# A decoder with two expert layers: the first expert layer turns its sorted tiles four at a time, runs its shared experts last and splits its weights on GpSimd

## The chip, the cores and the metric

The program runs on one core of a Trainium2 chip: one launch computes the whole decoder. The metric is the time of the device in microseconds (us). The engines are TensorE (PE; its loading of weights is shown apart as PEld), VectorE (DVE), ScalarE (ACT), GpSimd (POOL) and SyncE, whose queue (SPq) issues nearly all plain transfers. Each engine runs its instructions in order, and they wait for each other by semaphores.

## What is computed

A batch of 32 sequences of 64 tokens (2048 tokens, 256 features) goes through six blocks: a rotary recurrence, a cross attention, a first expert layer, a linear attention, a quantised cross attention and a second expert layer. The change touches the third alone. What that one computes, with `x` after a layer norm without weights:

```python
score = sigmoid(xn @ wa)                                  # 16 routed experts
val, idx = top_k(score, 2); val = val / val.sum(-1)
y_e = gelu(xn @ g_e + gb_e) * (xn @ w1_e + b1_e)           # [tokens, 128]
out_e = y_e @ w2_e + b2_e
x = x + xn + out_shared0 + out_shared1 + sum(val_k * out_(idx_k))
```

(`x + xn` since the layer's input is added again inside it.) Each token passes through its two chosen routed experts and through both shared ones.

## The kernel before

The stage is `experts_top2`. Tokens stand in 16 tiles of 128 (`NT`), in four blocks of 512 (`NBLK`, `TPB` = 4 tiles in a block). Products run in f16 with every operand split in a high part (scaled by 1024) and a low part: `split_product` is six matmuls, high by high, high by low and low by high, each over two halves of the features.

**Norm** (`RowNorm`): VectorE takes the moments of 16 tiles, ScalarE the square root (L904), and then, for each block b, VectorE writes `xn`, ScalarE its high part (L907) and VectorE its low part (`low`, L884) into `rows`, which lie in `xnT`. SyncE turns each finished block with one transposing DMA into `xh` or `xl` (L916) and copies it to `rows_dram` (L917).

**Routing** (`Dispatch`): TensorE's logits, ScalarE's sigmoid (L982), VectorE's choice of two experts (`vector_choose`), counts by TensorE (`tensor_place`) and places by VectorE (`vector_place`, to L1057). The routed work is sorted: each expert's tokens fill whole tiles of 128 rows, 48 tiles in all (`TILES`), in 12 quads of four. `vector_hot` and `tensor_list` make, for the first and the second choice in turn, the list `token` of which token sits in which row (L1075 to L1080), and `vector_experts` the expert of each tile.

**Weights**: 18 experts (16 routed, 2 shared) come through three staging slots (`Wgu`, `Wd`). ScalarE writes high parts (`split_high`, L1228 and L1229), VectorE low parts (`weights_low`, L1330 and L1331), from the staged f32 in one operation each. The order is written out by hand: the two shared experts first, then two experts after each shared step.

**Shared experts**: eight steps (2 experts by 4 blocks): `shared_up` (12 matmuls of 512 columns), `gate` and `hidden` (gelu on ScalarE, product on VectorE), high and low part of the result (`hidden_high`, `low`), `shared_down` (4 tiles by 4 matmuls of 256 columns, of which the fourth adds a bias: `ones3` by `b2r`, 3 partitions each), and `add` into `X`. These steps run while the weights of the routed experts still arrive and while the routing is computed.

**Routed experts**: GpSimd gathers each of the 48 tiles from `rows_dram` into one of four one-tile buffers `got` (`RING`, L1212), SyncE turns it into one of two quad buffers `XG` (L1188), and a gather into a buffer waits for the turn out of it. Per quad TensorE loads four expert numbers (`value_load`) and runs 48 matmuls of 128 columns (`routed_up`) and 16 of 256 (`routed_down`). ScalarE and VectorE empty the result into `y` (`take`), and SyncE keeps it in `y_dram` (`keep`). After the twelfth quad GpSimd gathers 32 tiles back into eight buffers `G` (L1220), and VectorE adds each, weighted, into `X` (L1382).

## Time and profile before

| | us |
|---|---|
| median of 3 runs (lowest, highest) | 2793.87 (2790.25, 2794.61) |
| the profiled execution, its own time | 2792.5 |
| its span | 2790.4 |
| this stage, from its first DMA issue to the end of its last operation | 475.8 to 754.0 |
| of that, until the first shared matmul | 475.8 to 518.3 |
| the shared steps | 518.3 to 593 |
| the twelve routed quads | 593.7 to 707.5 |
| gathering back and adding | 707.5 to 754.0 |
| mean granted clock of TensorE over the span, of full speed | 0.786 |

Times in the rows below are microseconds from the span's start. In a timeline row the first number is the start and the second the duration. For a row of several instructions (x4, x48) it is from the first start to the last end. A bracket says how long the engine had been idle before, and what ended that; "issue" means that nothing the profile shows did. A matmul's duration is longer than the distance to the next one, since they are pipelined: distances between starts tell TensorE's pace.

### The profile page before, as it was taken

How to read it: one execution, taken by the hardware profiler on the slowest of the kernel's cores; microseconds unless marked ns; L12 is line 12 of the kernel's file. 1: busy time of each engine (PE TensorE's matmuls, PEld its weight loads, DVE VectorE, ACT ScalarE, POOL GpSimd, SP SyncE). 2: the span in 40 equal slices, each digit the busy share in tenths (PEclk: the TensorE clock that was granted, in tenths of full speed). 3: DMA queues.
4: the chain of work that ended last, by engine and by line, in shares of the span. 5: the costliest groups of instructions: out<-in, count | busy, mean ns of one | idle time of the engine just before them, and what ended most of it. 6: DMA issues, size and time to landing. Idle time of an engine off the chain costs nothing. (4 is left out here: it accounts for less than half of the span.)

```text
span 2790.4 us, 44150 instructions
## 1 busy us (share of the span) xinstructions
PE 2067.5 (74%) x15822; PEld 1219.5 (44%) x15822; DVE 1742.4 (62%) x3183; ACT 1402.6 (50%) x1950; POOL 972.2 (35%) x882
## 2 busy tenths in 40 slices
PE   6783776487189999999946366666666549999998
PEld 3332554245067777777745122222222234444444
DVE  6996564742333333333365899999999645666665
ACT  4562332232043333333323488888888525666664
POOL 0000220023423223232313588888888600101010
PEclk9996777688589999999977555555555569999999
DMA  3000000468300000000000266666665400000001
GB/s 91 0 0 20 1 0 20 98 142 155 96 20 20 19 19 9 19 19 19 1 23 0 44 108 107 107 107 108 108 108 107 73 18 11 24 24 18 25 17 39
DMA packets 375874, 135.43 MB, mean 49 GB/s; under 512 B 318701, under 2 KB 372677, under 8 KB 375749
## 3 DMA queue, kind: packets, MB, share of 16 engines
q1 hardware_dynamic: 371909, 123.27, 21.5%
q0 software_dynamic: 3840, 10.49, 1.8%
q8 instruction: 79, 1.29, 0.2%
q14 instruction: 46, 0.38, 0.0%
HBM read 47.69 MB, written 10.49 MB: 21 GB/s over the span
## 5 line engine op out<-in xcount | busy, mean ns | idle before, releaser
L2008 POOL CAST xnT<-xl 128x2048 bf16<-128x2048 uint8 x256 | 484.0, 1891 | 15.5
L2043 PE MATMUL psum<-e_KT,e_QT 48*128 48x512 bf16 x1024 | 264.8, 617 | 271.9 <-DVE ctxT L2076 125.3
L2076 DVE TENSOR_SCALAR_CACHE_REDUCE ctxT<-psum,e_nsq 128x1024 f32<-128x1024 f32 x256 | 314.7, 1282 | 11.8 <-PE psum L2043 10.1
L2076 DVE TENSOR_SCALAR_CACHE_REDUCE e_Smore<-psum,e_nsq 128x1024 f32<-128x1024 f32 x256 | 314.7, 1281 | 1.4
L2094 ACT ACTIVATE xh<-e_Smore,e_ebias 128x2048 uint8<-128x2048 f32 x128 | 256.3, 2002 | 48.4 <-POOL e_ebias L2015 48.4
L2094 ACT ACTIVATE xh<-ctxT,e_ebias 128x2048 uint8<-128x2048 f32 x128 | 256.3, 2002 | 47.5 <-POOL e_ebias L2015 47.5
L1556 POOL TENSOR_TENSOR d_sq<-d_oS 128x512 f32<-128x512 f32 x64 | 99.2, 1549 | 420.9 <-ACT d_oS L1600 420.9
L116 PE MATMUL psum<-xh,d_WT 128*128 128x512 f16 x768 | 230.0, 382 | 2.6 <-DVE d_WT L1631 2.6
L2043 PEld LDWEIGHTS psum<-e_KT,e_QT 48*128 48x128 bf16 x1024 | 33.8, 107 | 401.6 <-DVE ctxT L2076 190.5
L1650 DVE TENSOR_TENSOR d_ACC<-psum,d_ACC 128x512 f32<-128x512 f32 x128 | 82.5, 686 | 171.0 <-PE psum L1704 171.0
L2053 PEld LDWEIGHTS psum<-e_Vi,xnT 128*128 128x128 bf16 x4096 | 119.5, 104 | 112.1 <-issue 104.3
L116 PE MATMUL psum<-xh,f_WA 128*128 128x512 f16 x544 | 152.7, 383 | 13.9 <-DVEq L2287 11.8
L2232 POOL TENSOR_TENSOR f_WA<-f_W,f_WA 128x512 f16<-128x512 f32 x17 | 19.7, 1159 | 407.6 <-ACT f_W2H L2252 407.6
L2303 DVE SCALAR_TENSOR_TENSOR X<-psum,f_route,X 128x256 f32<-128x256 f32 x272 | 112.8, 477 | 70.1 <-PE psum L2363 70.1
L2363 PE MATMUL psum<-f_W2H,f_hh 128*128 128x256 f16 x544 | 151.0, 278 | 3.1 <-DVE f_hh L2315 3.1
L2363 PE MATMUL psum<-f_W2L,f_hh 128*128 128x256 f16 (+1 forms) x544 | 150.8, 277 | 0.0
L2053 PE MATMUL psum<-e_Vi,xnT 128*128 128x16 bf16 x4096 | 131.3, 175 | 7.4 <-POOL xnT L2008 7.4
L1644 DVE SCALAR_TENSOR_TENSOR d_y<-d_gt,d_oS 128x512 f32<-128x512 f32 x64 | 44.3, 692 | 145.7 <-ACT d_oS L1600 145.7
L1704 PE MATMUL psum<-d_WoT,d_y 128*128 128x256 f32 x512 | 122.7, 382 | 5.9 <-DVE d_y L1644 5.7
L2266 ACT ACTIVATE f_h<-psum 128x512 f32<-128x512 f32 x68 | 40.6, 597 | 156.5 <-PE psum L116 156.5
L1584 ACT ACTIVATE d_kT<-psum 128x512 f32<-128x512 f32 x64 | 38.2, 597 | 159.3 <-PE psum L116 159.3
L238 PE MATMUL psum<-ident,ln_xn 128*128 128x128 f32 x160 | 31.2, 374 | 114.8 <-DVE ln_xn L204 114.8
(359 smaller groups left out, 4660.8 us busy)
## 6 DMA issues: line engine op xcount, KB each, us to landing
kept_y<-c_y SPq DMA_DIRECT2D x12, 512.0 KB
d_Wn<-in_L_attn_w_qkv SPq DMA_DIRECT2D x16, 384.0 KB, 3.2
f_W<-in_L_ffn_w_routed SPq DMA_DIRECT2D x32, 176.0 KB, 2.5
xl<-xh SPq DMA_TRANSPOSE x256, 3.0
ctx_rows<-in_ctx SPq DMA_DIRECT2D x1, 2048.0 KB, 8.7
X<-in_x SPq DMA_DIRECT2D x1, 2048.0 KB, 14.1
c_Wgu<-in_L_ffn_rg SPq DMA_DIRECT2D x16, 128.0 KB, 2.3
c_Wgu<-in_L_ffn_rw SPq DMA_DIRECT2D x16, 128.0 KB, 2.4
```

Of the source, the lines that this page charges most:

```text
L116: mm = pe.matmul(out, lhsT(a, k), rhs(b, k), start=(n == 0), stop=(n == len(terms) - 1))
L1556: pool.tensor_tensor(sq[:, :], o, o, ALU.mult).then_inc(squared, 1)
L1644: dve.scalar_tensor_tensor(y[:, :], gt[:, q % 2, :], 1.0, oS[:, q % 2, :], ALU.add, ALU.mult).then_inc(yready, 1)
L1650: last = dve.tensor_tensor(a2, m.bank[6 + half][:, :], a2, ALU.add)
L1704: mm = pe.matmul(m.bank[6 + j // 2][:, (j % 2) * D:(j % 2 + 1) * D], y[:, j * P:(j + 1) * P], WoT[:, slot, :], start=True, stop=True)
L2008: pool.tensor_copy(PT[:, sl, :], P8[:, sl, :, :].rearrange("p c q -> p (c q)").bitcast(U8)).then_inc(unpacked, 1)
L2043: mm = pe.matmul(m.bank[pair_banks(c + odd) + q], QT[rows, n // 2, :], KTt[rows, n % H // 2, col:col + BLK], start=True, stop=True)
L2053: mm = pe.matmul(m.bank[6 + j // 8][:, j % 8 * HD:(j % 8 + 1) * HD], PT[:, n % SLOTS, k // 2 * 2 * P + k % 2:(k // 2 + 1) * 2 * P:2], Vi[: ...
L2076: dve.tensor_scalar(S32[sl][:, hf * HALF:(hf + 1) * HALF].rearrange("p (a b) -> p a b", a=2), m.psum[:, b:b + 2, :], nsq[:, n + odd:n + od ...
L2094: act.activation(e8[:, sl, :], S32[sl], ACT.Exp, bias=ebias[:, sl:sl + 1], scale=-1.0, accum_out=esum[:, n:n + 1]).then_inc(exped, 1)
L2303: last = dve.scalar_tensor_tensor(m.X[:, t, :], m.bank[4 + 2 * (q % 2) + j // 2][:, (j % 2) * D:(j % 2 + 1) * D], R.route[:, t, ds(e, 1)], ...
L2363: mm = pe.matmul(m.bank[4 + 2 * (q % 2) + j // 2][:, (j % 2) * D:(j % 2 + 1) * D], a, b, start=(n == 0), stop=(n == len(terms) - 1))
```

## The change

The diff, cut to its core (waits and helpers left out where the text below tells them):

```diff
@@ sizes and buffers
-    ORDER = [*range(NE, NE + SH), *range(NE)]
-    STAGES, RING, GSLOTS = 3, 4, 8
+    ORDER = [*range(NE + SH)]
+    STAGES, GOT, TURNED, GSLOTS = 4, 4, 3, 8
-        b2r = sb("b2r", [3, NE + SH, D], BF16)
-        ones3 = sb("ones3", [3, P], BF16)
-        got = sb("got", [P, RING, 2 * D], F16)
-        XG = sb("XG", [P, 2, TPB, 2 * KC, P], F16)
+        b2r = sb("b2r", [P, NE + SH, D], BF16)
+        ones = sb("ones_bf", [P, P], BF16)
+        got = m.xnT[:, :, :].rearrange("p a b -> p (a b)").bitcast(F16).rearrange("p (s j d) -> p s j d", s=GOT, j=TPB)
+        XG = sb("XG", [P, TURNED, TPB, 2 * KC, P], F16)
@@ SyncE
                 for b in range(NBLK):
+                    weights(STAGES + 2 * b)
                     norm.sync(sp, b)
+                    weights(STAGES + 2 * b + 1)
-                def turn(i):
-                    qd, j = divmod(i, TPB)
-                    sp.wait_ge(fetched[i % RING], 16 * (i // RING + 1))
-                    if qd >= 2:
-                        sp.wait_ge(gate_up, shared_steps + qd - 1)
-                    sp.dma_start_transpose(XG[:, qd % 2, j, :, :], got[:, i % RING, :]).then_inc(across[qd % 2 * TPB + j], 16)
+                def turn(qd):
+                    sp.wait_ge(fetched[qd % GOT], 16 * TPB * (qd // GOT + 1))
+                    if qd >= TURNED:
+                        sp.wait_ge(gate_up, qd - TURNED + 1)
+                    sp.dma_start_transpose(XG[:, qd % TURNED, :, :, :].rearrange("p t c q -> p (t c) q"),
+                                           got[:, qd % GOT, :, :].rearrange("p t d -> p (t d)")).then_inc(across[qd % TURNED], 16)
@@ GpSimd
+                pool.memset(ones[:, :], 1.0).then_inc(bias_clear, 1)
+                pool.memset(b2r[:, :, :], 0.0).then_inc(bias_clear, 1)
+                for n in range(NE + SH):
+                    e, slot = ORDER[n], n % STAGES
+                    pool.wait_ge(high, n + 1)
+                    pool.tensor_tensor(Wx[:, e, 1], Wgu[:, slot], Wx[:, e, 0], ALU.subtract)
+                    pool.tensor_tensor(WdL[:, e], Wd[:, slot], WdH[:, e], ALU.subtract).then_inc(split, 1)
@@ ScalarE
-                    act.activation(Wx[:, e, 0], Wgu[:, slot], ACT.Copy, scale=SPLIT)
-                    act.activation(WdH[:, e], Wd[:, slot], ACT.Copy, scale=SPLIT).then_inc(high, 1)
+                    act.activation(Wgu[:, slot], Wgu[:, slot], ACT.Copy, scale=SPLIT)
+                    act.activation(Wd[:, slot], Wd[:, slot], ACT.Copy, scale=SPLIT).then_inc(scaled, 1)
+                    act.wait_ge(scaled, n + 1)
+                    act.activation(Wx[:, e, 0], Wgu[:, slot], ACT.Copy)
+                    act.activation(WdH[:, e], Wd[:, slot], ACT.Copy).then_inc(high, 1)
+                for n in range(STAGES):
+                    split_high(n)
+                norm.scalar_sd(act)
+                for b in range(NBLK):
+                    norm.scalar_high(act, b)
+                    split_high(STAGES + 2 * b)
+                    split_high(STAGES + 2 * b + 1)
@@ VectorE
-                dve.wait_ge(loaded, 16 * NLOADS)
                 norm.vector(dve)
                 R.vector_split(dve)
+                dve.wait_ge(loaded, 16 * NLOADS)
                 biases()
-                weights_low(0)
...
+                        if e:
+                            add(q)
+                            dve.wait_ge(summed, q + 1)
+                            for n in range(q * TPB * TOP, (q + 1) * TPB * TOP):
+                                combine(n)
```

- The shared experts move behind the routed ones. After the routing come the twelve quads, then the eight shared steps, and after each block's second shared step VectorE does the block's `add` and its eight `combine` operations (the weighted additions of what was gathered back, L1382 before).
- Weights: routed experts come first, four staging slots. ScalarE scales each staged weight in place (two operations), waits for that, and copies the high parts (two more); GpSimd subtracts to get the low parts, ahead of all its gathers. VectorE has no weight work left. The loads of the fifth to the twelfth expert stand in SyncE's queue around the norm's four blocks, and ScalarE splits two experts after each block's high part, six more after the scores.
- Norm: VectorE no longer waits for the loads before its statistics.
- Gathers fill one of four quad buffers, laid over `xnT`; one transposing DMA turns four tiles into one of three `XG` buffers; TensorE waits once per quad for it. `G` lies over the norm's `xn`.
- `vector_hot` has two buffers for its one-hot tiles and no longer waits for the first list.
- The bias matmul's operands have 128 partitions, zeros below the three that carry numbers.

**SyncE's queue at the second block of the norm.** Before, the blocks follow each other, and the loads of further weights stand behind the last:

```order
L917 DMA kept_rows<-xnT 128x4x512
L916 DMA_TRANSPOSE xh<-xnT 128x16x128 [waits c_n_low]
L917 DMA kept_rows<-xnT 128x4x512
L916 DMA_TRANSPOSE xl<-xnT 128x16x128 [waits c_n_low]
L917 DMA kept_rows<-xnT 128x4x512
```

Now (`c_Wgu` and `c_Wd` are the staging slots):

```order
L918 DMA kept_rows<-xnT 128x4x512
L1167 DMA c_Wgu<-in_L_ffn_rg 128x2x128 [waits c_split]
L1167 DMA c_Wgu<-in_L_ffn_rw 128x2x128
L1169 DMA c_Wd<-in_L_ffn_rw 128x256
L1167 DMA c_Wgu<-in_L_ffn_rg 128x2x128 [waits c_split]
L1167 DMA c_Wgu<-in_L_ffn_rw 128x2x128
L1169 DMA c_Wd<-in_L_ffn_rw 128x256
L917 DMA_TRANSPOSE xh<-xnT 128x16x128 [waits c_n_low]
L918 DMA kept_rows<-xnT 128x4x512
```

Two experts' loads stand between two blocks, the first of them behind a turn that waits for VectorE's `low`.

**ScalarE's queue at the same place.** Before, four high parts in a row and then the router's:

```order
L904 ACTIVATE c_sd<-c_mom,c_eps 128x16 [waits c_n_moments]
L907 ACTIVATE xnT<-c_xn 128x4x256 [waits c_n_xn] x4
L980 ACTIVATE c_wa<-c_wa 128x32
```

Now, from the first high part to the second:

```order
L908 ACTIVATE xnT<-c_xn 128x4x256 [waits c_n_xn]
L1245 ACTIVATE c_Wgu<-c_Wgu 128x512 [waits c_w0]
L1246 ACTIVATE c_Wd<-c_Wd 128x256
L1248 ACTIVATE c_Wx<-c_Wgu 128x512 [waits c_scaled]
L1249 ACTIVATE c_WdH<-c_Wd 128x256
L1245 ACTIVATE c_Wgu<-c_Wgu 128x512 [waits c_w1]
L1246 ACTIVATE c_Wd<-c_Wd 128x256
L1248 ACTIVATE c_Wx<-c_Wgu 128x512 [waits c_scaled]
L1249 ACTIVATE c_WdH<-c_Wd 128x256
L908 ACTIVATE xnT<-c_xn 128x4x256 [waits c_n_xn]
```

Eight operations and two waits for transfers (`c_w0`, `c_w1`) stand between two high parts of the norm.

**VectorE's queue at the end of the stage.** Before, the last quad's `low` and `take` and then 32 additions, each with its wait for a gather (`c_back`):

```order
L1296 SCALAR_TENSOR_TENSOR c_hl<-c_h,c_hh 128x512 [waits c_hhigh]
L1311 COPY c_y<-psum 128x512 [waits c_kept1,c_downs]
L1382 SCALAR_TENSOR_TENSOR X<-c_G,c_val,X 128x256 [waits c_back0]
L1382 SCALAR_TENSOR_TENSOR X<-c_G,c_val,X 128x256 [waits c_combined,c_back1]
L1382 SCALAR_TENSOR_TENSOR X<-c_G,c_val,X 128x256 [waits c_back2]
```

Now the end of the first block's additions, the second block's shared steps and its first addition (`c_xn` is where `G` lies):

```order
L1339 SCALAR_TENSOR_TENSOR X<-c_xn,c_val,X 128x256 [waits c_combined,c_back7]
L1315 SCALAR_TENSOR_TENSOR c_hl<-c_h,c_hh 128x512 [waits c_hhigh]
L1304 SCALAR_TENSOR_TENSOR c_h<-psum,c_gus,c_gelu 128x512 [waits c_gelu]
L1315 SCALAR_TENSOR_TENSOR c_hl<-c_h,c_hh 128x512 [waits c_hhigh]
L1304 SCALAR_TENSOR_TENSOR c_h<-psum,c_gus,c_gelu 128x512 [waits c_gelu]
L1330 SCALAR_TENSOR_TENSOR X<-psum,X 128x512 [waits c_downs]
L1330 SCALAR_TENSOR_TENSOR X<-psum,X 128x512
L1339 SCALAR_TENSOR_TENSOR X<-c_xn,c_val,X 128x256 [waits c_back0,c_summed]
```

The low parts that TensorE's next shared products need stand behind eight additions that wait for gathers.

## Rows read from the trace of the kernel before

**Rows 1.** Busy time by stretch: stretch, its length, PE, PEld, DVE, ACT, POOL, PEclk, DMA share, GB/s

```profile
620.00:680.00 60.00, 49.52 (x430) 34.75 (x429) 15.62 (x40) 14.82 (x41) 24.40 (x25) 0.86 0.84 172
```

**Rows 2.** Timeline, start and norm: start, us, engine, line, operation, [idle before <-releaser]

```profile
475.82 0.39 SPq L1153 DMA_DIRECT2D c_wa<-in_L_ffn_wa  x1
...
486.91 0.63 ACT L1228 ACTIVATE c_Wx<-c_Wgu 128x512 f16<-128x512 f32 x1 [13.48 <-DMA c_tokid<-in_tokid]
...
495.52 1.06 ACT L907 ACTIVATE xnT<-c_xn 128x1024 f16<-128x1024 f32 x1 [1.74 <-DVE c_xn L892]
...
499.22 1.22 DVE L884 SCALAR_TENSOR_TENSOR xnT<-c_xn,xnT 128x1024 f16<-128x1024 f32 x1
500.46 1.88 SPq L916 DMA_TRANSPOSE xh<-xnT  x1
...
502.40 1.14 SPq L917 DMA_DIRECT2D kept_rows<-xnT  x1
```

**Rows 3.** DMA issues of the stage: KB each, median us from issue to landing

```profile
c_Wd<-in_L_ffn_rw SPq DMA_DIRECT2D x16, 128.0 KB, 2.6
```

**Rows 4.** Timeline, last expert layer: GpSimd's subtraction beside a small VectorE operation

```profile
2290.86 1.16 POOL L2232 TENSOR_TENSOR f_WA<-f_W,f_WA 128x512 f16<-128x512 f32 x1 [3.05 <-ACT f_W2H L2252]
...
2290.96 1.10 DVE L810 SCALAR_TENSOR_TENSOR f_wa<-f_wa 128x32 f16<-128x32 f32 x1 [6.12 <-ACT f_wa L801]
```

**Rows 5.** Timeline, from the router's scores to the expert list

```profile
518.48 0.38 ACT L982 ACTIVATE c_score<-psum 128x256 f32<-128x256 f32 x1 [10.31 <-PE psum L116]
...
530.38 0.19 DVE L1057 SCALAR_TENSOR_TENSOR c_row<-c_tile,c_slot 128x32 f32<-128x32 f32 x1
...
540.57 0.96 DVE L1075 TENSOR_TENSOR c_tilehot<-c_iota,c_tile 128x768 f16<-128x768 f32 x1 [2.67 <-PE psum L1087]
...
542.44 2.28 DVE L1080 TENSOR_TENSOR c_rowhot<-c_iota,c_row 128x2048 f16<-128x2048 f32 x1
...
549.54 0.23 DVE L1354 TENSOR_SCALAR c_hot<-c_te,c_tokid 16x48 f32<-16x48 f32 x1
```

**Rows 6.** First gather, landing times of the turns, first routed matmuls

```profile
555.48 1.47 POOL L1212 DMA_INDIRECT c_got<-kept_rows,c_token  x1 [105.11 <-DVE c_token L1094]
...
DMA to landing us min/median/max: 2.7/5.0/9.4
...
593.74 4.46 PE L116 MATMUL psum<-c_XG,c_Wx 128*128 128x128 f16 x48 [4.62 <-issue]
```

**Rows 7.** Waits of GpSimd from 600 to 700: us in total, times, longest us

```profile
POOL c_got L1212 <- DMA c_XG<-c_got: 48.5, 19, 7.7
```

**Rows 8.** Timeline, TensorE: two of the quads that met no late transfer

```profile
609.77 4.80 PE L116 MATMUL psum<-c_XG,c_Wx 128*128 128x128 f16 x48 [1.63 <-issue]
...
635.39 4.43 PE L116 MATMUL psum<-c_XG,c_Wx 128*128 128x128 f16 x48 [1.19 <-issue]
```

**Rows 9.** Timeline, TensorE: a down product's four matmuls, and two of another layer

```profile
661.19 0.27 PE L1401 MATMUL psum<-c_WdL,c_hh 128*128 x1
661.30 0.27 PE L1402 MATMUL psum<-c_WdH,c_hl 128*128 x1
661.50 0.28 PE L1403 MATMUL psum<-c_b2r,c_ones 3*128 x1
...
2355.02 0.27 PE L2363 MATMUL psum<-f_W2H,f_hh 128*128 128x256 f16 x1
2355.23 0.28 PE L2363 MATMUL psum<-f_W2L,f_hh 48*128 48x256 f16 x1
```

**Rows 10.** Timeline: a shared up product, and the end of the stage

```profile
575.33 2.76 PE L116 MATMUL psum<-xl,c_Wx 128*128 128x512 f16 x12
...
707.13 0.39 PE L1403 MATMUL psum<-c_b2r,c_ones 3*128 x1
...
711.95 0.94 POOL L1220 DMA_INDIRECT c_G<-kept_y,c_home  x1 [22.81 <-DMA kept_y<-c_y]
...
753.54 0.48 DVE L1382 SCALAR_TENSOR_TENSOR X<-c_G,c_val,X 128x256 f32<-128x256 f32 x1 [0.77 <-DMA c_G<-kept_y,c_home]
```

More of the change, by code:

```diff
@@ L924, with __init__ @@
     NE = 16
-    def __init__(self, m, tag, own, norm, top, tiles, scale):
+    def __init__(self, m, tag, own, norm, top, tiles, scale, width=P):
         self.m, self.norm, self.top, self.tiles, self.scale = m, norm, top, tiles, scale
+        self.width, self.groups = width, tiles * P // width
         def sb(n, s, dt=F32):
@@ L1059, in vector_experts @@
     def vector_experts(self, dve):
-        c, NE, tiles = self.c, self.NE, self.tiles
+        c, NE, tiles = self.c, self.NE, self.groups
         shape = (P, tiles, NE)
@@ L1196, in _ @@
                 for qd in range(QUADS):
-                    for j in range(TPB):
-                        turn(qd * TPB + j)
-                    if qd >= 2:
-                        keep(qd - 2)
-                for qd in range(QUADS - 2, QUADS):
+                    turn(qd)
+                    if qd >= TURNED:
+                        keep(qd - TURNED)
+                for qd in range(QUADS - TURNED, QUADS):
                     keep(qd)
@@ L1297, in low @@
                                              ALU.mult, ALU.subtract).then_inc(hlow, 1)
-                def add(q):
-                    dve.wait_ge(downs, q + 1)
-                    for half in range(2):
-                        t = q * TPB + 2 * half
-                        x2 = m.X[:, t:t + 2, :].rearrange("p t d -> p (t d)")
-                        ins = dve.scalar_tensor_tensor(x2, m.bank[4 + half][:, :], R.scale, x2, ALU.mult, ALU.add)
-                    ins.then_inc(summed, 1)
                 def take(qd):
-                    dve.wait_ge(downs, NBLK + qd + 1)
+                    dve.wait_ge(downs, qd + 1)
                     if qd >= 2:
@@ L1312, in take, with add, combine @@
                                     m.bank[y_bank(qd) + 1][:, :]).then_inc(evac_dve, 1)
+                def add(q):
+                    dve.wait_ge(downs, QUADS + q + 1)
+                    for half in range(2):
+                        t = q * TPB + 2 * half
+                        x2 = m.X[:, t:t + 2, :].rearrange("p t d -> p (t d)")
+                        ins = dve.scalar_tensor_tensor(x2, m.bank[y_bank(QUADS + q) + half][:, :], R.scale, x2,
+                                                       ALU.mult, ALU.add)
+                    ins.then_inc(summed, 1)
+                def combine(n):
+                    t, k = divmod(n, TOP)
+                    dve.wait_ge(back[n % GSLOTS], 16 * (n // GSLOTS + 1))
+                    if k:
+                        dve.wait_ge(combined, n)
+                    dve.scalar_tensor_tensor(m.X[:, t, :], G[:, n % GSLOTS, :], R.val[:, t, k:k + 1], m.X[:, t, :],
+                                             ALU.mult, ALU.add).then_inc(combined, 1)
                 def biases():
-                    dve.memset(ones3[:, :], 1.0)
                     dve.wait_ge(bias_high, 1)
@@ L1458, in _ @@
                 for part in range(2):
-                    mm = pe.matmul(m.bank[6][:, 2 * P + part * TILES:2 * P + (part + 1) * TILES], gub[:, part, :], hot[:, :],
+                    mm = pe.matmul(m.bank[5][:, part * TILES:(part + 1) * TILES], gub[:, part, :], hot[:, :],
                                    start=True, stop=True)
                 mm.then_inc(tables, 1)
-                for s in range(3, shared_steps):
-                    if s + 1 < shared_steps:
+                pe.wait_ge(split, NE + SH)
+                pe.wait_ge(bias_moved, 16 * 3)
+                pe.wait_ge(bias_clear, 2)
+                pe.wait_ge(table_in, 2)
+                pe.wait_ge(R.told, 1)
+                now = experts(0)
+                routed_up(0, now)
+                for s in range(QUADS):
+                    if s + 1 < QUADS:
+                        after = experts(s + 1)
+                        routed_up(s + 1, after)
+                    else:
+                        shared_up(s + 1)
+                    routed_down(s, now)
+                    now = after
+                for s in range(QUADS, QUADS + shared_steps):
+                    if s + 1 < QUADS + shared_steps:
                         shared_up(s + 1)
                     shared_down(s)
-                pe.wait_ge(split, NE + SH)
-                pe.wait_ge(summed, NBLK)
-                now = experts(0)
-                routed_up(0, now)
-                for qd in range(QUADS):
-                    if qd + 1 < QUADS:
-                        after = experts(qd + 1)
-                        routed_up(qd + 1, after)
-                    routed_down(qd, now)
-                    now = after
 def lightning_attention(nc, m, w):
```

224 lines of the change are left out of this document (91 added, 133 removed).

## The prediction

> **What bounds the kernel now.** The change stays inside one stage of 278 us, so I read that stage alone: first its timeline from the start, then the waits of the routed quads, then the timeline of its end.
>
> At the start VectorE and ScalarE stand still for 11 us behind all loads: the stage's first DMA issues at 475.8 and ScalarE's first operation runs at 486.9 [rows 2]. The norm then moves at VectorE's pace; scores end at 518.9 [rows 5]. From there to 593.7 routing, weight splitting and shared products share the engines, and the routed quads begin when the last shared block is summed, long after the token list is there (first gather 555.5) [rows 6].
>
> In the routed quads GpSimd waits half of the time for a turn to empty one of its four one-tile buffers (48.5 of 100 us) [rows 7]. It is a ring: gather, land, turn, land, gather again. TensorE starts twelve quads in 113.8 us (593.7 to 707.5), 9.5 each, but quads that met no late transfer came (635.39 - 609.77) / 3 = 8.54 us apart [rows 8]. The 16 DMA engines are 84% busy [rows 1], so they aren't far from being the next bound.
>
> After the last down product (707.5) the stage is one thread: 4.4 us until the results are kept, then 32 gathers, one every 1.25 us, with an addition 2.7 us behind each (711.95 + 31 x 1.25 + 2.7 = 753.5), and the end at 754.0: 46.5 us in which TensorE does nothing [rows 10].
>
> **The change, part by part.** I follow one path through the changed stage: scores, token list, first routed matmul, last down product, end.
>
> *Start.* ScalarE now splits four experts first. The first lands about 2.6 us after its issue [rows 3], near 480.4. One expert costs two passes over 128x512 and 128x256: 0.61 us or so for the larger operation [rows 2], 0.4 for the smaller, partly overlapped, twice, with a wait between: 2.0. Four end at 488.4; square root with its table load 1.6, reciprocal and the first block's four subtractions 1.7, so the first high part starts at 491.7 instead of 495.5. VectorE's statistics (6 us from 476) are hidden under this. The first low part, 3.7 behind as before, ends at 496.6: 4 us gained.
>
> *The norm's blocks* then lose it again. The loads of one of the two experts that ScalarE splits between two high parts stand in SyncE's queue behind the block's turn, and that turn waits for VectorE's low part. So one block leads to the next through everything: turn 1.9 and row copy 1.1 [rows 2], three load issues 1.4, landing 2.6 [rows 3] (7.0 so far), split 2.0, high part 1.1, low part 1.2 [rows 2]: 11.3 us a block, where the low parts of before came 4 us apart or closer. The fourth low part ends at 496.6 + 3 x 11.3 = 530.5. Behind it a further load and split (9.0), biases and router weights (0.9), logits (3.2) and scores (0.4): 544.0, which is 25 us later than 518.9 [rows 5].
>
> *Routing* gets shorter, since nothing is interleaved. Score to places took 530.57 - 518.86 = 11.7 with one hidden product (0.75) in it: 11.0. One set of one-hot tiles takes 540.57 to 544.72, twice 8.2, and they no longer wait for TensorE (2.67 us idle before that row). From there to 549.77 are 5.1, of which a low part and two weight pairs are 2.6: 2.5. List 0.3. Sum 22.0, token list at 566.0 [rows 5].
>
> But GpSimd splits weights at the same time. Where it does so beside a VectorE operation that reads two operands from SBUF, that operation waits: 128x32 elements took 1.10 us beside a subtraction of 1.16 [rows 4], where one of the same size takes 0.19 [rows 5]. Six experts are left when the scores come, some 12 us of GpSimd nearly without a gap, over ten such small operations of the choice and the places. Between nothing and 10 x 0.9 = 9; I take half, 5, and 2 more for the norm's four low parts. Token list at 573. The Trainium skill speaks against this part of the change: "SBUF — State Buffer", section "SBUF: two separate sides", has the pair of ports that VectorE and GpSimd share as an exclusive lock for a whole instruction. By that rule each meeting costs the rest of GpSimd's 1.16, which is the upper end, 9, and the trace agrees in the one place quoted.
>
> *To the first routed matmul*: GpSimd starts 0.9 after the list [rows 6], four gathers are 3 x 1.25 + 2.7 = 6.5 [rows 10], the turn's landing 5.0 (2.7 to 9.4) [rows 6]: 585.4. Splitting ends some 10 us before, so nothing else holds it. That is **8.3 us earlier** than 593.7.
>
> *The quads.* With sixteen tiles of gathers ahead and three turned buffers the ring is gone, and the pace should be TensorE's 8.54. A second thing comes with the wide bias operands. At the high clock (2.4 GHz) matmuls of 256 columns start 0.11 apart, but the bias matmul on 3 partitions starts 0.20 behind its neighbour; the last expert layer shows the same 0.21 for a 48-partition matmul of one type with its neighbours, so the number of partitions makes it, not bf16 [rows 9]. The way back costs as much. With 128 partitions 0.2 per tile goes, 0.8 per quad: 7.7. Per quad the DMA engines need 0.84 x 8.8 = 7.4 [rows 1], so they just fit. Twelve quads are 92.4, and 2 more for filling the pipe and because a shared up product (2.76) [rows 10] now stands ahead of the last down product: 94.5 against 113.8, **19.3 us less**. Last down product at 679.9.
>
> *The end.* Gathers back start 4.4 later as before. VectorE reaches its first eight additions about 10 us after the last routed product and stays in them until the eighth gather has landed: 4.4 + 7 x 1.25 + 2.7 + 0.5 = 16.4. Behind them stand the low parts for TensorE's next down product, and from then on a block goes in one chain: low part 0.7, down 1.8, up 2.8, down 1.8, add 1.3, eight additions 4.2, semaphores 0.2: 12.8 us at the high clock, above the 10 us that eight gathers need. TensorE idles some 4 us in each; before, the quads with their shorter stalls ran at a granted 0.86 [rows 1], so some of it will be at the low level. With all three products at half speed (1.2 GHz) a block is 18.9. I take 15, nearer to the high clock. End: 16.4 + 3 x 15 = 61.4 against 46.5, **14.9 us more**. So the eight shared steps, which had 75 us of their own, cost 15 at the end instead; most of what they free is already used up by the slower start.
>
> **Sum**: -8.3 - 19.3 + 14.9 = -12.7. The profiled execution took 2792.5 (span 2790.4), the median of three runs 1.4 more, so its time becomes 2779.8 and the median 2781.2.
>
> Bounds. Start: no blocking and quick landings -9, late landings +16 (below). Quads: 7.25 (no gap beyond a single microsecond between products) to 8.54: -5 and +10. End: 12.8 to 18.9 a block, -7 and +12. All short ends together give -33, all long ones +25; neither is likely at once.
>
> **Rivals.**
> 1. *All covers hold*: no blocking, high clock at the end, short quads. For it: in the quads the ports are hardly contested. Against: the idle time of TensorE at the end is certain. -24 to -33, 2761 to 2770.
> 2. *The transfers set the pace*: the DMA engines' 84% is as much as they give beside gathers of scattered rows, and quads stay 9.2 apart. +18, so 2799. Against: quads of 8.4 to 8.7 us did come.
> 3. *The wide bias brings nothing*: 0.8 per quad and 1.6 per block of the end stay, 10 + 5 us, 2796. The rows with 48 partitions speak against it. The Trainium skill has both views: "TensorE: Matmul & The Clock Gate", "Step-by-step: what each phase is for", says that the row count does not matter for a product's time, and "TensorEngine Tiling (Array Packing)", "Key Properties", that changing the tiling mode drains TensorE; the 0.20 against 0.11 agrees with the second.
> 4. *Slower: the norm's chain is longer.* Each expert load queues behind a turn and a row copy of 512 KB on the same rings. A turn landed after up to 9.4 us [rows 6]; then the load lands 9.4 + 2.6 = 12.0 after the turn's issue and not 7.0. Four times 5 us: +20, so 2801. It decides for slower by over 0.2% from 4.6 us more per block, (12.7 + 5.6) / 4. Against: now the turns are 11 us apart and meet empty rings, while 9.4 was measured among gathers.
>
> **How the numbers follow.** The forecast, 2770 to 2788, gets 0.54; rival 1 0.14, rival 2 0.08, rival 3 0.05, rival 4 0.12, and 0.07 is left for mixtures on both sides. A measurement of this kernel can tell about 0.2%, 5.6 us, from no change. Faster by more: the forecast, rival 1 and some of the mixtures, 0.70. Within: rival 3, half of rival 2 and the rest, 0.15. Slower: rival 4, the other half of 2 and a mixture, 0.15. The range leaves out the far ends of rivals 1, 2 and 4: 2764 to 2798.
>
> **What would show it.** In the profile after: ScalarE's high parts of the norm about 11 us apart, with waits for a weight load before the second split; scores near 544; VectorE operations of 0.2 us that take about 1; the first routed matmul near 585; up products 7.7 apart with no wait for a turn, and bias matmuls 0.11 behind their neighbours; GpSimd far ahead of the turns; after the last quad 16 us and three blocks of 13 to 19 us. The prediction is wrong if the high parts come at 4 or at 16 us, if quads stay above 9, or if the end takes under 50 us.

## The result, and the profile after

The change makes the kernel **slower**: 2809.6 us median (2805.9 to 2810.5) against 2792.1 before, ratio 1.0061 with a 95% interval of 1.0044 to 1.0079. The profiled execution took 2805.9 us, its span 2804.1, at a granted clock of 0.785 (before 0.786). The forecast was 2781.2, with a range of 2764 to 2798.

Start: the timeline of the changed kernel (start, length in us, engine, line, operation, idle time before it and who ended it), from the norm's turns to the first routed matmul. It answers to [rows 2, 5, 6].

```profile
496.38 2.04 SPq L917 DMA_TRANSPOSE xh<-xnT  x1
...
504.30 0.63 ACT L1245 ACTIVATE c_Wgu<-c_Wgu 128x512 f32<-128x512 f32 x1 [10.96 <-DMA c_Wd<-in_L_ffn_rw]
...
508.54 1.85 SPq L917 DMA_TRANSPOSE xh<-xnT  x1
...
546.45 0.38 ACT L987 ACTIVATE c_score<-psum 128x256 f32<-128x256 f32 x1 [2.38 <-PE psum L116]
...
573.38 0.19 DVE L1100 CAST c_token<-psum 128x48 uint32<-128x48 f32 x1
...
587.86 5.33 PE L116 MATMUL psum<-c_XG,c_Wx 128*128 128x128 f16 x48 [13.27 <-DMA c_XG<-xnT]
```

The turns are 12.1 us apart and ScalarE waits for a weight load in each block: the chain through everything is there. Scores, token list and first routed matmul came at 546.5, 573.4 and 587.9 (forecast 544, 573, 585.4).

Quads: TensorE's timeline, answering to [rows 8]. "x48" is one up product.

```profile
594.65 1.14 PE L116 MATMUL psum<-c_XG,c_Wx 128*128 128x128 f16 x8 [1.47 <-issue]
596.19 0.27 PE L116 MATMUL psum<-c_XG,c_Wx 128*128 128x128 f16 x2 [0.39 <-issue]
598.31 0.37 PE L116 MATMUL psum<-c_XG,c_Wx 128*128 128x128 f16 x2 [1.85 <-issue]
599.74 0.26 PE L116 MATMUL psum<-c_XG,c_Wx 128*128 128x128 f16 x1 [1.06 <-issue]
...
606.11 0.27 PE L116 MATMUL psum<-c_XG,c_Wx 128*128 128x128 f16 x1 [1.84 <-issue]
608.93 0.27 PE L116 MATMUL psum<-c_XG,c_Wx 128*128 128x128 f16 x1 [2.56 <-issue]
611.72 0.27 PE L116 MATMUL psum<-c_XG,c_Wx 128*128 128x128 f16 x1 [2.52 <-issue]
613.12 3.25 PE L116 MATMUL psum<-c_XG,c_Wx 128*128 128x128 f16 x29 [1.14 <-issue]
622.69 4.34 PE L116 MATMUL psum<-c_XG,c_Wx 128*128 128x128 f16 x48 [0.58 <-issue]
631.18 4.54 PE L116 MATMUL psum<-c_XG,c_Wx 128*128 128x128 f16 x48 [2.29 <-issue]
...
701.28 4.88 PE L116 MATMUL psum<-c_XG,c_Wx 128*128 128x128 f16 x48 [2.27 <-issue]
```

Two things are to be seen. The second up product **drips**: it begins at 594.65, and for 18 us its matmuls come singly or in pairs, 0.7 us or a multiple of it apart, "issue" before each, so that TensorE waits for nothing the profile shows. And the quads behind it are still 8.7 us apart ((701.28 - 622.69) / 9). The first product's signal drips too: that product ended at 593.2, and ScalarE's gelu, which waits only for it, began at 613.3. Meanwhile GpSimd issued 28 gathers without a pause; this is the last of them, and then ScalarE:

```profile
608.64 0.95 POOL L1229 DMA_INDIRECT xnT<-kept_rows,c_token  x1 [0.30 <-issue]
...
613.30 1.28 ACT L1264 ACT_TABLE_LOAD   x1 [38.42 <-remote]
```

The down products did become shorter. TensorE's timeline, answering to [rows 9]: all four matmuls of a tile are now 0.11 apart, a tile 0.44 instead of 0.64.

```profile
627.20 0.27 PE L1397 MATMUL psum<-c_WdH,c_hl 128*128 x1
627.31 0.27 PE L1398 MATMUL psum<-c_b2r,c_ones_bf 128*128 x1
627.42 0.27 PE L1395 MATMUL psum<-c_WdH,c_hh 128*128 x1
```

End: VectorE's timeline, the four additions of a block and the last combining, answering to [rows 10].

```profile
721.14 1.29 DVE L1330 SCALAR_TENSOR_TENSOR X<-psum,X 128x512 f32<-128x512 f32 x2 [0.28 <-issue]
...
740.58 0.75 DVE L1304 SCALAR_TENSOR_TENSOR c_h<-psum,c_gus,c_gelu 128x512 f32<-128x512 f32 x1 [8.76 <-ACT c_gelu L1259]
741.25 1.27 DVE L1330 SCALAR_TENSOR_TENSOR X<-psum,X 128x512 f32<-128x512 f32 x2
...
755.26 1.29 DVE L1330 SCALAR_TENSOR_TENSOR X<-psum,X 128x512 f32<-128x512 f32 x2 [0.28 <-PE psum L1398]
...
766.51 1.29 DVE L1330 SCALAR_TENSOR_TENSOR X<-psum,X 128x512 f32<-128x512 f32 x2 [3.23 <-PE psum L1398]
767.84 4.03 DVE L1339 SCALAR_TENSOR_TENSOR X<-c_xn,c_val,X 128x256 f32<-128x256 f32 x8
```

| Part, us of the profile | before | after | difference | forecast |
|---|---|---|---|---|
| first routed matmul | 593.7 | 587.9 | -5.9 | -8.3 |
| first routed matmul to last down product | 113.8 | 124.6 | +10.8 | -19.3 |
| last down product to last combining | 46.5 | 59.4 | +12.9 | +14.9 |
| sum | | | +17.8 | -12.7 |

The spans differ by 13.7, so the later stages took some 4 us less in this profile than in that of before. The medians differ by 17.5, as much as the stage does. The miss of 30 us lies in the middle row.

### The profile page after: what moved, and what is told of

Same layout as the page of the kernel before. It is cut to its first block and busy times, and to the rows that moved or that the text cites. A ratio compares the mean times of both kernels' runs of the same rounds, so it can differ in the third digit from the quotient of the medians.

```text
span 2804.1 us, 44119 instructions
## 1 busy us (share of the span) xinstructions
PE 2048.5 (73%) x15822; PEld 1226.7 (44%) x15822; DVE 1742.2 (62%) x3146; ACT 1419.1 (51%) x1986; POOL 1013.6 (36%) x920
## 5 line engine op out<-in xcount | busy, mean ns | idle before, releaser
L2289 DVE TENSOR_TENSOR f_pr<-psum,f_h 128x512 f32<-128x512 f32 x68 | 47.0, 692 | 108.9 <-ACT f_h L2262 108.9
```

The source lines that it names most:

```text
L2289: dve.tensor_tensor(pr[:, st % 2, 0, :], m.bank[1][:, :], h1[:, st % 2, 0, :], ALU.mult).then_inc(product, 1)
```

## Experiments

For the drip I set three theories against each other. A: a run of gathers on GpSimd holds TensorE back. B: ScalarE's first Gelu table load is late and holds the rest. C: the instructions of the new stage arrive late. For the pace of 8.5: TensorE's own work with registers, or the transfers. In the table, "up to up" is the time from the first to the last routed up matmul, and the last column counts gathers issued without a pause during the quads; both come from the timelines. Each ratio is to runs of the kernel before that were made beside that kernel, with medians of 2790.0 to 2792.2, so a difference between two kernels of the table is uncertain by 1 to 2 us.

| Kernel | median us | ratio to before (95%) | up to up | drips in quads, us | gathers in a row |
|---|---|---|---|---|---|
| before | 2792.1 | | 106.6 | none | 1 to 4 |
| after | 2809.6 | 1.0061 (1.0044 to 1.0079) | 118.0 | 18 | 28, then 4 |
| gather_paced | 2788.6 | 0.9993 (0.9984 to 1.0003) | 99.4 | none | 4 to 8 |
| gelu_early | 2786.3 | 0.9985 (0.9975 to 0.9995) | 96.2 | none | 36, then 4 |
| act_copy | 2810.1 | 1.0065 (1.0045 to 1.0085) | 116.3 | 15 | 28, then 4 |
| static_loads | 2775.3 | 0.9945 (0.9923 to 0.9967) | 83.6 | none | 44, then 4 |
| static | 2764.5 | 0.9906 (0.9886 to 0.9926) | 74.4 | none | 36, then 4 |
| multi | 2802.7 | 1.0037 (1.0021 to 1.0053) | 109.0 | 18, 5 | 28, 8, 4 |
| multi_paced | 2793.3 | 1.0002 (0.9992 to 1.0011) | 102.7 | 7, 4, 4 | 4 to 8 |
| norm_first | 2790.1 | 0.9993 (0.9984 to 1.0003) | 116.3 | 15 | 28, then 4 |
| norm_paced | 2778.5 | 0.9939 (0.9923 to 0.9956) | 110.8 | 4, 2, 4 | 4 to 8 |
| combined | 2769.8 | 0.9913 (0.9896 to 0.9929) | 97.0 | 8, 4, 4 | 4 to 8 |
| tail16 | 2809.7 | 1.0062 (1.0045 to 1.0078) | 119.8 | 18, 3 | 28, then 4 |
| before_wide | 2783.3 | 0.9966 (0.9951 to 0.9982) | 103.2 | none | 1 to 4 |
| before_wide_one | 2781.3 | 0.9957 (0.9940 to 0.9974) | 103.4 | none | 1 to 4 |
| after_spaced | 2787.0 | 0.9985 (0.9975 to 0.9996) | 98.5 | none | none |
| combined_spaced | 2761.2 | 0.9888 (0.9871 to 0.9904) | 95.3 | none | none |
| combined_spaced16 | 2754.8 | 0.9864 (0.9847 to 0.9880) | 93.8 | none | none |

**gather_paced** (GpSimd):

```diff
+                    if 2 <= qd and j == 0:
+                        pool.wait_ge(across[(qd - 2) % TURNED], 16 * ((qd - 2) // TURNED + 1))
```

> The changed kernel with one wait more on GpSimd: from the third quad on, the gathers of quad q are issued only when the transfer that turns quad q-2 has landed, so that it no longer issues 28 in a row at the start. Theory A (the unbroken run of gathers from 574.5 to 609.6 us holds back TensorE's instructions and the other engines' start): the second up product runs at the pace of the first (5.3 us), the third begins near 603 instead of 622.7, and the kernel gains 15 to 20 us (2790 to 2795 by the profile's clock). Theory B (ScalarE's first Gelu table load is late for a reason of its own) and theory C (the instructions of the new stage arrive late, whatever GpSimd does): the third up product still begins near 622, and the time stays within 2 us of 2806, or is up to 5 us longer if the pacing starves the turns.

The drip went, and 21 us with it, as A wanted. **gelu_early** (ScalarE, after the last split):

```diff
+                act.activation(warm[:, :], norm.eps[:, :], ACT.Gelu)
```

> The changed kernel with one more ScalarE instruction: a Gelu of one column right after the last weight split and before the bias table, so that the Gelu table is loaded 15 us before the first routed quad (nothing reads its result). Theory B (the table load at 613.3 is what holds the second and third up product): hidden(0) comes near 595, the third up product near 603, 15 to 20 us gained. Theories A and C: the first gelu itself still waits until about 613, and at most 1.3 us, the load itself, is gained.

It went here too, 23 us, which A didn't expect, since GpSimd issued 36 gathers in a row. That looked like B. **act_copy** is the same line with ACT.Copy.

> The changed kernel with one ScalarE instruction more after the last weight split, as in gelu_early, but a Copy of one column instead of a Gelu, so that no table is loaded early. gelu_early took the 20 us stall away. If the early table did that, the stall comes back here: third up product near 622, 2806 us. If the stall hangs on the moment at which TensorE's first 'up product done' signal falls into the stream of gathers, so that any small shift can avoid it, it may be gone here as well (2786 to 2788), and then neither the table nor the run of gathers alone is its cause.

The drip was back: 2810.1. But the next two kernels keep the late table load and have no drip, and multi, below, has the early one and drips, so B falls. Neither the table nor the length of the run alone decides.

**static_loads** and **static** (TensorE) take constants for the experts of the tiles, so their output is another one; static also leaves out the loads. The diff is static's, without the down product's addresses, which change alike:

```diff
-                    return [pe.value_load(R.expert[0:1, i:i + 1], min_val=0, max_val=NE - 1)
-                            for i in range(qd * TPB, (qd + 1) * TPB)]
+                    return [i * NE // TILES for i in range(qd * TPB, (qd + 1) * TPB)]
-                                lambda x, k: Wx[:, ds(es[j], 1), x, k, part, :].rearrange("p a f -> p (a f)"),
+                                lambda x, k: Wx[:, es[j], x, k, part, :],
```

> The changed kernel with the expert of each tile a constant of the program in the matmuls' addresses (tile i takes expert i/3 rounded down, so the output is that of other experts), while TensorE still loads the four expert numbers of each quad and doesn't use them. If the four loads are what makes the 2.5 us pause before each up product, the pause and the pace of 8.5 to 8.7 us per quad stay nearly as they are. If the register instruction ahead of each matmul sets the pace, the up product becomes shorter than 4.4 us and the quad falls to about 8.0. If transfers or VectorE set the pace (rival 2 of the prediction), it stays at 8.5 too, but then the next kernel shows it as well.

> As the one before, and without the loads: the expert of each tile is a constant, TensorE loads no expert number (the output is that of other experts). If TensorE's own register work sets the pace, the pause of 2.5 us before each up product goes and the quad falls from 8.5 to 6.0 to 7.4 us (the transfers' bound that the prediction took was 7.4), 10 to 25 us over the quads. If transfers set it, the quads stay at 8.5 and TensorE waits for c_across instead of 'issue'. The stall of the second up product tells theory A from C as well: without loads and register instructions, it should stay if GpSimd or instruction fetch causes it.

Neither drips. For static that was not expected: I had written that the stall should stay if GpSimd or the fetching of instructions caused it. Their numbers settle the pace alone. TensorE's timeline, static_loads first, then static:

```profile
602.04 2.84 PE L116 MATMUL psum<-c_XG,c_Wx 128*128 128x128 f16 x48 [1.76 <-issue]
608.37 2.84 PE L116 MATMUL psum<-c_XG,c_Wx 128*128 128x128 f16 x48 [1.75 <-issue]
```

```profile
604.70 2.84 PE L116 MATMUL psum<-c_XG,c_Wx 128*128 128x128 f16 x48
609.13 2.84 PE L116 MATMUL psum<-c_XG,c_Wx 128*128 128x128 f16 x48
```

A quad that nothing holds up takes 8.5 us with registers, 6.3 with loads alone and 4.4 with neither. The register instruction that computes an address ahead of two thirds of the matmuls stretches an up product from 2.84 to 4.3 us, and the four loads make a pause of 1.75 (1.6 to 3.3 in the changed kernel, mostly 2.2, with the address instructions of the down product before it). TensorE's sequencer, not its array, set the pace, in the kernel before as well; "issue" ahead of each up product was its trace. The sequencer's instructions in the changed kernel (ns, shortest, median and longest):

```profile
L1440 PEldq TENSOR_LOAD <-c_expert x43: 293/298/1019, 592.0 to 699.7; - x43
L1440 PEldq FUSED_REGOPS  x42: 146/151/151, 592.3 to 699.4; - x42
```

With its two parts of bounds check a load comes 0.64 us behind the one before. The Trainium skill, "DMA: Bandwidth & Descriptors", section "Latency and other measured facts", gives a tensor load a floor of about 0.6 us and says that the compiler unrolls it four times to amortize it. The trace has 0.30 for the load itself, half of that floor, and 0.64 only with the bounds check; the next kernel shows that one load for four values does save time.

In static the transfers are the next bound, 28.4 us of waits for a turn in all, 13.2 of them ahead of the first product.

**multi** (gelu_early, and one load for a quad):

```diff
+                    return nc.values_load_multi_w_load_instructions(
+                        R.expert[0:1, qd * TPB:(qd + 1) * TPB], [mybir.EngineType.PE], min_val=0, max_val=NE - 1)[1]
```

> gelu_early with the four expert numbers of a quad fetched by one load instruction of TensorE in place of four. static_loads against static gave 1.75 to 2.0 us per quad for the four loads. If each load's 0.30 us and its own bounds check make the pause, it falls from 2.3 us to 1 to 1.3 us, the quad from 8.5 to 7.4 to 7.6 us, and the kernel to 2773 to 2777 us. If the transfers are the next bound they show here first: the quads stay above 8 us and TensorE waits for c_XG.

The quads without a drip were 7.5 us apart, as expected, but the drip was back, and a second one came. TensorE's timeline of the second, and GpSimd's last gather of that run:

```profile
638.70 1.16 PE L116 MATMUL psum<-c_XG,c_Wx 128*128 128x128 f16 x12 [1.26 <-issue]
640.01 0.22 PE L116 MATMUL psum<-c_XG,c_Wx 128*128 128x128 f16 x1 [0.16 <-issue]
...
644.21 0.27 PE L116 MATMUL psum<-c_XG,c_Wx 128*128 128x128 f16 x1 [1.15 <-issue]
644.91 1.33 PE L116 MATMUL psum<-c_XG,c_Wx 128*128 128x128 f16 x11 [0.43 <-issue]
```

```profile
642.28 0.95 POOL L1230 DMA_INDIRECT xnT<-kept_rows,c_token  x1 [0.30 <-issue]
```

**multi_paced** is multi with gather_paced's wait, **norm_paced** the same on norm_first.

> multi (one load for four expert numbers, Gelu table early) with the pacing of gather_paced: no gather of quad q before the transfer that turns quad q-2 has landed. In multi TensorE's matmuls came one by one, 0.7 us or a multiple of it apart, at 597 to 616 and at 638 to 645 us, both times while GpSimd issued gathers without a pause. Theory A (such a run of gathers can hold TensorE back; whether it does in a given kernel hangs on the moment): both places go, and the quads keep 7.5 us, so that the kernel comes to 2772 to 2780. If the drip has another cause, at least one of them stays, and the time is above 2785.

> norm_first with the pacing of gather_paced. norm_first has the drip at 577 to 593 us. Theory A: the drip goes, the third up product comes at 584 to 586 instead of 602.6, and the kernel gains 16 to 18 us on norm_first: 2770 to 2775. The rival (the drip belongs to the first routed products, whatever GpSimd does) leaves 2788 to 2792.

Both gained 9 and 12 us, but not the whole, and both kept drips of 2 to 7 us: pacing by quads doesn't end them, it only shortens the runs. gather_paced had been spared as gelu_early had. What all drips share shows over the eight kernels that have any. I count 19 of them, each of at least two late matmuls in a row (single ones are left out): 17 begin within a run of gathers and two small ones of the stage's end 0.8 and 1.4 us behind one, and every one ends after its run's last gather, 2.8 to 4.0 us after runs of 16 and 28, 1.0 to 1.9 after runs of four and eight. None lies elsewhere. Four kernels with larger turns and the same kind of gathers have no drip.

**norm_first** (order on ScalarE and SyncE):

```diff
-                    weights(STAGES + 2 * b)
+                    weights(STAGES + b)
                     norm.sync(sp, b)
-                    weights(STAGES + 2 * b + 1)
...
+                norm.scalar_high(act, 0)
+                split_high(STAGES)
+                for b in range(1, NBLK):
+                    norm.scalar_high(act, b)
```

> The changed kernel with the start in another order: ScalarE does the four high halves of the norm and the router's weights ahead of the splits of experts 5 to 17, and SyncE issues the four turns of the norm with one expert's loads between them in place of two, none of which waits. The prediction took the norm's chain of weight load, split, high half, low half and turn as 11.3 us per block (12.1 measured). Without it the four turns should follow one another at 3 to 4 us, the scores come at 512 to 520 instead of 546, the first routed matmul at 553 to 562 instead of 588, if the splits (1.8 us each on ScalarE, 13 of them, and their loads) still end before the token list. Rival: the weights' loads, 4 slots deep, then end after the routing and hold the first routed matmul to 570 to 580. The 20 us stall of the second up product may stay or go with the shift; with it the kernel should be at 2772 to 2796, without it at 2755 to 2775.

The norm's turns came 5.4 to 5.9 us apart, the scores at 519.4 instead of 546.5, but the token list only at 553.6, 34.2 behind them instead of 26.9. GpSimd's splits now lie beside all of the routing, 28.8 of 33.6 us busy, where they had 11.0 of 27.0, and VectorE's one-hot tiles of 2048 elements took 2.75 and 3.23 instead of 2.28. So 27 us ahead became 18.6 at the first routed matmul, and the drip of 15 us was there.

**tail16** gives the gathers of the end 16 slots and combines each block one block later (the new place of the slots and the last block's loop are left out):

```diff
-    STAGES, GOT, TURNED, GSLOTS = 4, 4, 3, 8
+    STAGES, GOT, TURNED, GSLOTS = 4, 4, 3, 16
-                            for n in range(q * TPB * TOP, (q + 1) * TPB * TOP):
+                            for n in range((q - 1) * TPB * TOP if q else 0, q * TPB * TOP):
```

> The changed kernel with 16 slots for the gathers of the end, laid over the rows of the norm (which are dead there), in place of 8, and the combining of block q done after block q+1 is added. Nothing else is touched, so the stall and the quads should stay as in the changed kernel. If the end is long because GpSimd waits for slots and VectorE combines a block before it may add the next, it falls from 59.4 us to 47 to 51 (32 gathers of 1.25 us after the last y is kept, plus the last combines) and the kernel to 2794 to 2799. If the end is set by the chain of the shared experts (up product, gelu, hidden, down, sum), it stays at 57 to 60.

Nothing gained, and the end showed that a drip doesn't need registers. TensorE's timeline, a shared up product whose addresses are constants, in a run of 16 gathers (721 to 741):

```profile
735.42 0.38 PE L116 MATMUL psum<-xl,c_Wx 128*128 128x512 f16 x1
736.70 0.58 PE L116 MATMUL psum<-xl,c_Wx 128*128 128x512 f16 x1 [0.91 <-issue]
738.10 1.03 PE L116 MATMUL psum<-xl,c_Wx 128*128 128x512 f16 x2 [0.81 <-issue]
740.89 1.44 PE L116 MATMUL psum<-xl,c_Wx 128*128 128x512 f16 x3 [1.76 <-issue]
```

**before_wide** is the kernel before with only the bias rows on 128 partitions. **before_wide_one** also has the single load, without the check.

> The kernel before with the bias rows of the down product on 128 partitions (125 of them zero) in place of 3, and nothing else of the change. The prediction took 0.20 us off each tile's four down matmuls, 0.8 us per quad, 9.6 us over 12 quads. In the changed kernel the 0.20 us was gone and the quad no shorter, since the pause before the next up product grew. If TensorE's register work sets the pace of this kernel too, the quads keep 8.5 us or gain at most 0.3 (2789 to 2793 in all); if the array's own time counts in part, they gain up to 0.8 each (2781 to 2785).

> The kernel before with two edits: its bias rows on 128 partitions, and the four expert numbers of a quad by one load without the check. No other part of the change. before_wide gained 8.9 us, 5 of it ahead of the quads. multi took the undisturbed quad from 8.5 to 7.5 us. If that adds here: 2770 to 2774, as much as the combined kernel, and its gathers, in twos and fours, show no drip. If the transfers, 16 turns where the changed kernel has 4, or the ring of 4 tiles set the pace once TensorE is faster (rival 2), it stays at 2778 to 2783 and TensorE waits for c_XG in most quads.

before_wide gained 8.9 us. Counted from the stage's start, which came 1.2 later in its profile, 6.1 of it lie ahead of the quads, near the 6.4 that 32 tiles of 0.20 make in the eight shared steps; I had left this part out in what I expected of it. The quads gained 3.4, 0.3 each, and those that met no late transfer stayed 8.5 apart. before_wide_one gained no more in the quads (103.4): TensorE's waits there, us in total, times, longest:

```profile
PE psum L116 <- DMA c_XG<-c_got: 24.3, 17, 4.9
```

That is rival 2, but in the kernel with one-tile turns. The larger turns pay with four loads as well, where no drip takes it back: 96.2 in gelu_early against 103.2 in before_wide. With one load, combined's quads, drips and all, took 97.0 against 103.4.

**combined** is norm_first, gelu_early, gather_paced and the single load without the check.

> The changed kernel with four things together: the norm's turns ahead (norm_first), the gathers paced (gather_paced), the Gelu table early, and the four expert numbers of a quad by one load without the bounds check on TensorE (the list is clamped before). If the gains add (18.6 us at the first routed matmul, some 20 from the drip, 1 us per quad from the load and 0.3 to 0.6 more without the check), the kernel comes to 2755 to 2765, and beats both. If the transfers become the bound once TensorE's register work shrinks, the quads stay at 7.5 and TensorE waits for c_XG: 2762 to 2770.

2769.8: it beats both, but by less than the gains added up to (2755 to 2765), with drips of 8, 4 and 4 us in its quads.

**after_spaced** and **combined_spaced** put a pause between two gathers of tokens (and, ahead of the first, a wait for the weight splits, which are long done):

```diff
+                    if i:
+                        pool.wait_ge(idled, i)
+                    pool.memset(Wgu[:, 0], 0.0).then_inc(idled, 1)
```

> The changed kernel with a memset of 128 x 512 of a dead tile on GpSimd between two gathers, each waited for by the next, and nothing else: the gathers of the tokens come some 1.8 to 2.2 us apart in place of 1.25, in as long a run. If the drip needs GpSimd to issue gathers without a pause, it goes (2786 to 2792, with 1 to 4 us for the slower gathers at the start). If it comes with any gather in flight while TensorE fetches its instructions or signals, it stays, and the run being longer, the time is 2805 or more.

> combined with the same memset between two gathers. combined has drips of 5.7, 3.5 and 4.6 us at 573, 589 and 634 us, each in a burst of 4 to 8 gathers. If pauses end them, it gains up to 12 us (2758 to 2762), less what the slower first gathers cost (8 x 0.7 us at most, 5.6). If not, it is 0 to 6 us slower than combined: 2770 to 2776.

GpSimd's timeline in after_spaced: gathers 1.66 us apart in place of 1.25.

```profile
577.87 0.97 POOL L1231 DMA_INDIRECT xnT<-kept_rows,c_token  x1 [0.17 <-issue]
578.82 0.55 POOL L1235 MEMSET c_Wgu<- 128x512 f32 x1
579.54 0.95 POOL L1231 DMA_INDIRECT xnT<-kept_rows,c_token  x1 [0.16 <-issue]
```

48 gathers follow one another like this, and no drip is left, in this kernel nor in the two combined ones (their gathers of the end, 16 and 32 in a row and not spaced, set off none either). after_spaced is 22.6 us faster than the changed kernel by one memset of 0.55 us, and combined_spaced 8.7 faster than combined. So the drip goes with gathers issued back to back: 8 of the 12 kernels with larger turns and no memset between gathers have it, none of the 3 with it. That makes the pause its likely cure, not a proven one, since four kernels have no drip without a memset; if the builds were independent, three more would do so by chance once in 27.

**combined_spaced16** adds tail16.

> combined_spaced with the end of tail16 (16 slots, combining one block late). In tail16 the end didn't shorten, and TensorE dripped for 7.1 us at 735 to 743 in a run of 16 gathers. The end's gathers are not spaced here. If the end is GpSimd's 32 gathers (40 us) plus a tail, it should be 4 to 8 us shorter than in combined_spaced; if the drip in its run of 16 or the chain of the shared experts sets it, it is within 2 us of it.

The median fell by 6.4 us; the end, from the last routed down product to the last combining, by 5.1 (57.2 to 52.1), where tail16 with its drip had 64.2. This is the fastest kernel, 2754.8 us, 1.4% below before. Its TensorE waits in the quads almost only for turns, 13.5 us of that ahead of the first product:

```profile
PE psum L116 <- DMA c_XG<-xnT: 32.5, 11, 13.5
```

Its quads come 8.1 us apart on average ((657.88 - 568.84) / 11), slower than the 7.5 in multi: here the turns set the pace. Whether the slower gathers, their pacing or the transfers hold the turns back was not separated.

## Why the prediction was wrong, step by step

- *Start*: right. A block took 12.1 us for 11.3 forecast, 3 x 0.8, and the first routed matmul came 2.5 late. The token list stood 26.9 behind the scores; 22.0 and 5 of blocking make 27. The blocking can be read by itself: from the first operation of the choice to the last of the places VectorE took 15.8 us (546.86 to 562.63), against 10.9 before without the hidden product, so 4.9 more; half of the bounds was a guess that hit. It isn't limited to operations with two operands, as the prediction had it: the conversion c_idxf<-c_idx, which reads one, took 1.07 us beside a subtraction and 0.23 before. In norm_first, with splits beside all of it, the blocking cost 7.3 more.
- *The quads*: this step failed, by 30.1 us. From the first to the last up matmul the forecast stands for 88.0 (94.5 less the 6.5 that follow). Without the drip it is 96.2, as in gelu_early; with it 118.0. So **21.8 us** are the drip (18.6 or 19.5 if gather_paced or after_spaced stands for the kernel without it), a mechanism that was in no rival and a term that the sum had at nothing, and **8.2** the pace: 8.51 in place of 7.7. There I had taken 0.8 us off each quad because TensorE's array saved it. The pause ahead of the next up product grew from 1.2 and 1.6 us [rows 8] to 2.2: the sequencer was behind anyway. I had read "issue" as small change, and it was the bound. Rival 3 had this outcome, with the wrong reason.
- *The gap of the 3-partition bias*: right in size. The 0.20 is gone in the changed kernel, and before_wide shows some 6 us of it on the shared steps, whose addresses need no register. The Trainium skill, "TensorE: Matmul & The Clock Gate", "Step-by-step: what each phase is for", says of the weight load that the row count does not matter, and of the stream that it takes as many cycles as there are columns. Neither gives the 0.20 against 0.11 of a 3-row product among 128-row ones, which the change took away; here the measurement decides. Where the sequencer is the bound it hardly counts either way.
- *The ring gone*: right. GpSimd ran as far ahead as its buffers let it, and just that made the long run of gathers.
- *The end*: right, 59.4 for 61.4, and the chain is the one described: the first eight additions ended 16.7 us after the last routed down product (16.4 forecast), and the three blocks took 17.4, 14.0 and 11.3 for three times 15. The first holds a small drip at 738 that I didn't know of, so that the sum is nearer than its parts.
- *The sums*: they hold but for the bounds. Late landings stand there with +16, while rival 4 works out four times 5, +20; with 20 all long ends make +29, not +25.
- *Rivals*: 4 gave 2801 and had the sign, but not by its mechanism: the norm's chain was 0.8 us per block longer, not 5. 1 is excluded. 2 belongs to the kernel before.

Without the drip the changed kernel takes 2786 to 2787 (gelu_early, after_spaced): 5 us above the forecast, inside its range, and faster than before by 0.15%, which is hardly more than nothing against the 0.45% forecast. That it comes so near is in part luck: 8.2 us of pace were missing there too, and an end of 57.2 for 61.4 made up half of them.

## What to carry to other kernels

Where an engine's gaps are put down to "issue", count its register loads and address instructions before you take array time off it: here a quad's sequencer work was 8.5 us and its matmuls' 4.4, and one load for four values was worth 1 us. When a change lets GpSimd run ahead, look at what its unbroken run of gathers does to other engines, and try a short pause between two of them. A kernel that shows a stall only in some builds has a cause that a small shift can hide: test a second neutral shift, as act_copy here, before you believe that the first one was a cure.

## What was unexpected of the hardware

While GpSimd issues indirect gathers 1.25 us apart (0.95 busy, 0.30 idle), TensorE can fall to one instruction per 0.7 us or a multiple, up to 2.8, for as long as the run lasts and 1 to 4 us more, and its signal to other engines is held as well: 20 us in the changed kernel. It comes with dynamic and with constant addresses and in runs of 4 to 28, and not always: runs of 36 and 44 showed none, nor did gather_paced's of 4 and 8. With 0.7 us between gathers none of 144 set it off. What starts it stays open. Among the instruction fetches of queue q8, one of 16 KB lies at 593.9 in the changed kernel, but also one at 594.7 in gelu_early, and each had landed within 1 us. In combined the drips of 589.3 and 634.3 have no such fetch in the 9 us before them; the next ones come at 591.5 and 643.5. That speaks against theory C without excluding it. The Trainium skill, "SBUF — State Buffer", section "SBUF: two separate sides", has VectorE and GpSimd alone wait for one another and TensorE never; if that holds for the buffer's ports, the drip sits somewhere else. No run here shows where.
